# Two attentions and a mixture of experts on one core: the join of the attentions put into attention 1, memsets put off, and attention 1 written out

## The chip, the core and the metric

The kernel runs on one core of a Trainium2 chip. The core has TensorE (PE, matmuls; its weight loads are shown as PEld), VectorE (DVE), ScalarE (ACT), GpSimd (POOL) and SyncE (SP, which here issues DMAs). Each engine works through its own instructions in program order and waits for others by semaphores. The metric is the device time of one execution in microseconds.

## The reference, cut to what matters

Everything is float32. The input x is 4 batches of 256 tokens of 256 elements.

```python
x = x + layernorm(attention1(layernorm(x)))      # 16 heads of 16, causal
x = x + layernorm(ffn(layernorm(x)))
def ffn(f):
    h = rmsnorm(f, ln1_w)
    # attention 2: 32 query heads of 128 on 4 key heads, rotary positions, causal
    x = f + softmax(mask(rope(h @ Wq) @ rope(h @ Wk).T / sqrt(128))) @ (h @ Wv) @ Wo
    t = rmsnorm(x, ln2_w)
    # 8 of 32 experts for each token, and a shared expert
    return x + moe(t) + shared(t)
```

## The kernel before

Products are kept exact to float32 by splitting each operand into a high and a low part, and `three` (L71) issues three matmuls for each product (L73, L74, L75). ACT makes the high part by a copy out of PSUM, DVE the low part by a subtraction.

Four blocks of the program follow each other, and all engines meet between two of them:

- `prepare` (L252 on): loads x and the weights, normalises x (`Norm`: `moments` on DVE at L142 to L150, `roots` on ACT at L164, `factors` on DVE at L170 and L173, `apply` on ACT at L185), turns tokens so that features are on partitions (`Turn`: transposes L212 on PE, high part L222 on ACT, low part L231 on DVE) into `act_t`, and zeroes buffers on POOL (L303 to L318).
- attention 1 (`AttentionA`, tags `a_`): 8 iterations (a batch and half of its heads each) of 4 slots (a pair of heads each). The work of a slot is a software pipeline: scores of pair P, transposed probabilities of P-2, values of P-4, the output projection of P-5, and units (projections of the next iteration). Iterations 0, 1, 6 and 7 are written out; 2 to 5 are a loop (`Fori`) whose body holds two. Five slots of drain end it. From its third iteration on, a projection reads the turned tokens from `src_t`, into which SP copies a batch by DMA (L947).
- attention 2 (`AttentionB`, tags `b_`): 16 iterations (a key head and a batch) of 4 slots, all written out. A slot needs its queries three slots ahead: projection (PE), raw copy (ACT, L1119), exchange of halves by two DMAs (SP, L1127), rotation in two steps (POOL, L1147 and L1151), high part (ACT, L1156) and low part (DVE, L1161). SP first issues the weights of the next key head on the same queue (L1487).
- the experts, not touched.

Between the attentions stands the join, for each batch b: normalise attention 1's sum (statistics, then L185 on ACT), add it to x (L1639 on DVE), statistics of the new x, the feed-forward input in two scalings (POOL, L1680, keeps one in `acc` as what attention 2 is added to; ACT, L185, makes the other), and `Turn` into `act_t`. Before, all of this but the first statistics of batches 0 to 2 stands at the start of attention 2, in the order that `pipeline` gives, with attention 2's first projections laced in. The rows go into `prob`, so attention 2's probabilities must not come before them.

A sqrt and an exp need different tables in ACT, and the compiler puts an ACT_TABLE_LOAD before the first use after a change.

## Times and profile before

| | us |
|---|---|
| median of 3 runs | 960.92 (959.73 to 962.18) |
| the profiled execution | 961.15 |
| its span, first to last instruction | 959.1 |
| prepare, to the start of attention 1 | 25.4 |
| attention 1 | 25.4 to 182.7 |
| start of attention 2, to its first scores | 183.0 to 213.4 |
| attention 2 and the experts | 213.4 to 959.1 |

Busy over the whole span: PE 870.1 us (91%), DVE 624.5 (65%), ACT 569.9 (59%), POOL 456.0 (48%). These shares are means over stretches with different limits; a row for one stretch tells more. In a row of a timeline the first number is the start in us from the span's start, the second the time in us that the instructions took together, x their count, and the bracket the idle time of the engine before them and what ended it.

### The profile page before, as it was taken

Reading aid. Unit: us, or ns where it says so; the run is one execution under the profiler, and the core shown is the slowest. Engines: PE = TensorE matmul, PEld = TensorE weight load, DVE = VectorE, ACT = ScalarE, POOL = GpSimd, SP = SyncE. Lnnn points to the kernel's source line nnn. Section 1 sums busy time; section 2 is a strip of 40 time slices with the busy share of each in tenths; the row PEclk is TensorE's granted clock in tenths of the full one; section 3 lists DMA queues with packets and bytes.
Section 4 is the critical chain, followed back from the end, with each engine's and each line's share of the span. In section 5 each row is a group of like instructions: output and inputs, shape, how many; then the busy total and the mean of one; then the engine's idle time right before and its main releaser. Section 6 shows DMA issues by size and latency. Waiting matters only on the chain. (4 is left out here: it accounts for less than half of the span.)

```text
span 959.1 us, 18782 instructions
## 1 busy us (share of the span) xinstructions
PE 870.1 (91%) x6108; PEld 804.9 (84%) x6108; DVE 624.5 (65%) x1620; ACT 569.9 (59%) x1572; POOL 456.0 (48%) x480
## 2 busy tenths in 40 slices
PE   4699999467999999999999999978999999999994
PEld 2589899456999998999899999967888888888884
DVE  7366666656788788877778777765545444444546
ACT  4788888455776766667666676654443334333333
POOL 5633334156766776777766777720222222221221
PEclk9999999778999999999999999997999999999998
DMA  6000100311114111141111111200433333333321
GB/s 210 23 1 24 44 23 1 99 34 38 41 46 134 44 44 35 44 134 45 33 46 40 40 46 45 51 1 17 142 116 110 99 114 103 110 115 115 104 88 44
DMA packets 50246, 63.34 MB, mean 66 GB/s; under 512 B 5728, under 2 KB 36064, under 8 KB 50176
## 3 DMA queue, kind: packets, MB, share of 16 engines
q1 hardware_dynamic: 49088, 61.41, 21.9%
q10 hardware_dynamic: 1088, 1.05, 0.3%
q8 instruction: 37, 0.61, 0.3%
q14 instruction: 33, 0.27, 0.1%
HBM read 41.86 MB, written 1.18 MB: 45 GB/s over the span
## 5 line engine op out<-in xcount | busy, mean ns | idle before, releaser
L637 POOL TENSOR_TENSOR b_prob<-b_prob,b_rsum 128x256 f32<-128x256 f32 (+1 forms) x128 | 104.9, 840 | 111.0 <-DVE b_rsum L619 111.0
L73 PE MATMUL banks<-act_t,b_w 128*128 128x256 f32 (+1 forms) x392 | 130.1, 332 | 1.9 <-DVE moe_hid L1994 1.0
L75 PE MATMUL banks<-act_t,b_w 128*128 128x256 f32 (+1 forms) x392 | 128.0, 327 | 0.0
L74 PE MATMUL banks<-act_t,b_w 128*128 128x256 f32 (+1 forms) x392 | 127.9, 326 | 0.0
L1898 ACT ACTIVATE moe_hid<-banks 128x512 fp32r<-128x512 f32 x66 | 39.5, 598 | 124.2 <-DVE banks L1989 124.2
L1298 ACT ACTIVATE b_prob<-banks,b_negmax 128x128 f32<-128x128 f32 (+1 forms) x256 | 103.6, 417 | 14.1 <-DVE b_negmax L1285 14.0
L1982 DVE TENSOR_TENSOR moe_gated<-banks,moe_share 128x512 f32<-128x512 f32 x66 | 45.6, 691 | 85.4 <-PE banks L75 81.8
L1156 ACT ACTIVATE b_qt<-b_work 128x512 fp32r<-128x512 f32 x64 | 40.4, 632 | 90.0 <-POOL b_work L1151 90.0
L1151 POOL TENSOR_TENSOR b_work<-b_work 128x512 f32<-128x512 f32 x64 | 86.6, 1353 | 9.5 <-DVE b_work L1139 0.4
L637 POOL TENSOR_TENSOR a_prob<-a_prob,a_rsum 128x256 f32<-128x256 f32 x64 | 51.6, 828 | 81.4 <-DVE a_rsum L619 81.4
L1147 POOL TENSOR_TENSOR b_work<-b_work,rope_t 128x512 f32<-128x512 f32 x64 | 83.2, 1300 | 7.9 <-DMA b_work<-b_work 7.9
L1285 DVE CUSTOM_DVE_ANT_0 banks<-banks,mask_neg 128x128 f32<-128x128 f32 (+1 forms) x256 | 83.6, 387 | 3.5 <-PE banks L75 1.0
L73 PE MATMUL banks<-b_kt,b_qt 128*128 128x128 f32 (+1 forms) x256 | 76.2, 298 | 8.1 <-issue 6.2
L73 PEld LDWEIGHTS banks<-act_t,b_w 128*128 128x128 f32 x392 | 76.4, 195 | 7.1 <-DVE moe_hid L1994 1.2
L75 PEld LDWEIGHTS banks<-act_t,b_w 128*128 128x128 f32 x392 | 75.8, 193 | 6.1
L74 PEld LDWEIGHTS banks<-act_t,b_w 128*128 128x128 f32 x392 | 76.2, 194 | 4.8
L73 PE MATMUL banks<-b_w,b_ot 128*128 128x256 f32 x256 | 73.1, 286 | 5.6 <-DVE b_ot L1342 5.6
L1994 DVE TENSOR_TENSOR moe_hid<-banks,moe_hid 128x512 fp32r<-128x512 f32 x66 | 45.6, 692 | 45.3 <-ACT moe_hid L1898 45.3
L1342 DVE TENSOR_TENSOR b_ot<-banks,b_ot 128x512 fp32r<-128x512 f32 x64 | 44.1, 689 | 44.8 <-ACT b_ot L1337 44.7
L75 PE MATMUL banks<-b_w,b_ot 128*128 128x256 f32 x256 | 72.4, 283 | 0.0
L74 PE MATMUL banks<-b_w,b_ot 128*128 128x256 f32 x256 | 72.3, 283 | 0.0
L1945 POOL TENSOR_TENSOR b_w<-b_w_raw,b_w 128x512 fp32r<-128x512 f32 x16 | 20.8, 1298 | 106.8 <-ACT b_w L1884 106.8
(229 smaller groups left out, 3041.4 us busy)
## 6 DMA issues: line engine op xcount, KB each, us to landing
b_work<-b_work SPq DMA_DIRECT2D x128, 128.0 KB, 2.3
moe_share<-gates SPq DMA_DIRECT2D x32, 512.0 KB, 3.6
b_w_raw<-in_b_wq SPq DMA_DIRECT2D x4, 1024.0 KB, 5.4
b_w_raw<-in_b_wo SPq DMA_DIRECT2D x4, 1024.0 KB, 9.1
a_src_t<-act_t SPq DMA_DIRECT2D x5, 512.0 KB, 2.9
moe_w_raw<-in_wg SPq DMA_DIRECT2D x16, 128.0 KB, 2.2
moe_w_raw<-in_wu SPq DMA_DIRECT2D x16, 128.0 KB, 2.3
moe_w_raw<-in_wd SPq DMA_DIRECT2D x16, 128.0 KB, 2.2
```

The source lines that it names most:

```text
L73: nc.tensor.matmul(out, w_lo, m_hi, start=start, stop=False, skip_group_check=skip)
L74: nc.tensor.matmul(out, w_hi, m_lo, start=False, stop=False, skip_group_check=skip)
L75: return nc.tensor.matmul(out, w_hi, m_hi, start=False, stop=stop, skip_group_check=skip)
L637: last = self.m.nc.gpsimd.tensor_tensor(rows, rows, rsum[:, :, t:t + 1].to_broadcast([PART, 2, width]), ALU.mult)
L1147: nc.gpsimd.tensor_tensor(sin, sin, self.q_table(1), ALU.mult).then_inc(self.sin_ready, 1)
L1151: nc.gpsimd.tensor_tensor(total, total, self.swp[:, P % 2, :], ALU.add).then_inc(self.q_added, 1)
L1156: self.m.nc.scalar.activation(self.qt[:, P % PAIRS, 0, :], self.cos_part[:, P % 2, :], ACT.Copy).then_inc(self.qt_hi, 1)
L1285: last = nc.vector.tensor_tensor_reduce(row, row, m.mask_neg[:, SEQ - width:SEQ], 1.0, -NEG, ALU.add, ALU.min, accum_out=self.negmax[:, p ...
L1298: last = nc.scalar.activation(self.prob[:, p, h, lo:lo + width], m.s_ps[:, h, lo:lo + width], ACT.Exp, bias=self.negmax[:, p % 2, t, h:h + ...
L1342: self.m.nc.vector.tensor_tensor(self.ot[:, p % 2, 1, :], self.m.o_ps[:], self.ot[:, p % 2, 0, :].bitcast(F32), ALU.subtract).then_inc(sel ...
L1982: nc.vector.tensor_tensor(gated[n][:], gu[n][1], share[par][:, n * half:(n + 1) * half], ALU.mult).then_inc(gated_done, 1)
L1994: nc.vector.tensor_tensor(hid[n][:, 1, :], gu[n][0], hid[n][:, 0, :].bitcast(F32), ALU.subtract).then_inc(hid_ready, 1)
```

## The change

It consists of four edits.

1. `prepare` zeroes only half of `q_stack` and the key stack. The rest of `q_stack` and the value buffer `v` are zeroed by POOL at the start of attention 1, and ACT waits for them (`zeroed`) before it first writes there.
2. The join is split up. Batches 0 and 1 are done within attention 1: `after(k)` is called behind each slot on each engine, k counting from -32 at the first slot of iteration 0 to -1 at the last of iteration 7, and 0 to 4 in the drain. Their rows lie in `q_stack` and the normalisation of attention 1's sum is POOL's for them. Batches 2 and 3 begin at attention 2's start and end in its slots 0 to 2 (the entries `"first"`); `Turn` uses banks 6 and 7 for them instead of 2 and 3.
3. Attention 1's loop is written out.
4. Its projections read `act_t` directly; `src_t` and the copies are gone.

```diff
-            nc.gpsimd.memset(m.b_w[:, 2 * B_W:4 * B_W].bitcast(F32), 0.0)
-            nc.gpsimd.memset(m.q_stack[:].bitcast(F32), 0.0)
+
+            nc.gpsimd.memset(m.q_stack[:, 0:NTT * HPI * PART].bitcast(F32), 0.0)
+            k_at = 2 * B_W + 2 * NTT * HPI * PART
+            nc.gpsimd.memset(m.b_w[:, k_at:k_at + NTT * HPI * STACK].bitcast(F32), 0.0)
...
-    COPIED = 3
-
     def src(self, it, part, c, t):
-        at = part * NC * SEQ + c * SEQ + t * PART
-        if isinstance(it, int) and it < self.COPIED:
-            at += self.batch(it) * SLOT
-            return self.m.act_t[:, at:at + PART]
-        return self.src_t[:, at:at + PART]
-
-    def wait_src(self, pe, it):
-        if not (isinstance(it, int) and it < self.COPIED):
-            pe.wait_ge(self.src_loaded, 16 * (it - self.COPIED + 1))
+        at = self.batch(it) * SLOT + part * NC * SEQ + c * SEQ + t * PART
+        return self.m.act_t[:, at:at + PART]
 
     def unit_bank(self, it, u):
...
-    def run(self, eng, slot, middles, after=None):
-
-
-        for it in range(2):
-            for p in range(PAIRS):
-                slot(eng, it, p)
-        for first, last in middles:
-            self.splitting = last <= self.ITS - NB
-            with eng.Fori(first // self.UNROLL, last // self.UNROLL) as step:
-                for k in range(self.UNROLL):
-                    self.parity = k
-                    for p in range(PAIRS):
-                        slot(eng, step * self.UNROLL + k, p)
-        for it in range(middles[-1][1], self.ITS):
+    def run(self, eng, slot, after=None):
+
+
+        for it in range(self.ITS):
             for p in range(PAIRS):
                 slot(eng, it, p, units=it < self.ITS - 1)
+                if after:
+                    after(PAIRS * (it - self.ITS) + p)
         for k in range(self.DRAIN):
...
+        if it == 0:
+            wait(act, self.zeroed, 1)
...
+            if it == 1:
+                wait(act, self.zeroed, 2)
...
+            nc.gpsimd.memset(self.v.rearrange("p a t h n -> p (a t h n)").bitcast(F32), 0.0).then_inc(self.zeroed, 1)
+            nc.gpsimd.memset(m.q_stack[:, NTT * HPI * PART:].bitcast(F32), 0.0).then_inc(self.zeroed, 1)
             nc.gpsimd.memset(m.acc[:], 0.0).then_inc(self.y_added, 1)
...
+            def after(k):
+
+                if k == -5:
+                    pool.wait_ge(self.qt_full, PAIRS * (self.ITS - 1))
+                    join.pool_attention(pool, 0)
+                if k == -4:
+                    join.pool_attention(pool, 1)
+                if k in (2, 3):
+                    join.gpsimd(pool, k - 2)
+
+            self.run(pool, self.slot_pool, after)
...
+            def after(k):
+                if k in (3, 4):
+                    if k == 3:
+                        pe.wait_ge(self.exp_done, 2 * PAIRS * self.ITS)
+                    join.turn.tensor(pe, k - 3)
+
+            self.run(pe, self.slot_pe, after)
...
+            def after(k):
+                if k == -6:
+                    m.norm_a.roots(act, 0)
+                    m.norm_a.roots(act, 1)
+                if k == 0:
+                    join.norm_f.roots(act, 0)
+                    join.norm_f.roots(act, 1)
+                    m.norm_a.roots(act, 2)
+                if k in (1, 2):
+                    join.act_input(act, k - 1)
+                if k in (3, 4):
+                    join.turn.scalar(act, k - 3)
+
+            self.run(act, self.slot_act, after)
...
+            def after(k):
+
+                if k in (-8, -7, -2):
+                    b = {-8: 0, -7: 1, -2: 2}[k]
+                    m.norm_a.moments(dve, b, lambda t: acc[:, t, :], arrived)
+                if k == -6:
+                    m.norm_a.factors(dve, 0)
+                    m.norm_a.factors(dve, 1)
+                if k in (-4, -3):
+                    join.dve_add(dve, k + 4)
+                if k == 1:
+                    join.norm_f.factors(dve, 0)
+                    join.norm_f.factors(dve, 1)
+                    m.norm_a.factors(dve, 2)
+                if k == 4:
+                    join.turn.vector(dve, 0)
+
+            self.run(dve, self.slot_dve, after)
+            join.turn.vector(dve, 1)
...
+        if it < NB:
+            wait(pe, self.join.turn.lo_done, it + 1)
...
+        if P == 0:
+            wait(pe, self.join.turn.lo_done, 3)
...
-            self.join.gpsimd(pool, 0)
-            self.join.gpsimd(pool, 1)
             self.pool_kv(pool, 0, self.KV0)
             self.pool_kv(pool, 0, self.KV1)
-            self.join.gpsimd(pool, 2)
             self.pool_rotate(pool, 0)
-            self.join.gpsimd(pool, 3)
             self.pool_rotate(pool, 1)
-            self.slots(pool, self.slot_pool, {})
+            join = lambda b: self.join.gpsimd(pool, b)
+            self.slots(pool, self.slot_pool, {("first", 0): ((join, 2),), ("first", 1): ((join, 3),)})
...
-            turn.tensor(pe, 0)
-            pe.wait_ge(turn.lo_done, 1)
             self.pe_kv(pe, 0, self.KV0)
-            turn.tensor(pe, 1)
             self.pe_kv(pe, 0, self.KV1)
             self.pe_queries(pe, 0)
-            turn.tensor(pe, 2)
             self.pe_queries(pe, 1)
-            turn.tensor(pe, 3)
             self.pe_kv(pe, 0, self.KT)
             self.pe_queries(pe, 2)
-            pe.wait_ge(turn.lo_done, NB)
+
+            def turn_h(b):
+                pe.wait_ge(*((self.raw_ready, 2) if b == 2 else (self.k_raw_ready, NTT)))
+                turn.tensor(pe, b)
...
+            join = self.join
+            join.act_attention(act, 2)
+            self.act_kv(act, 0, self.KV0)
+            m.norm_a.roots(act, 3)
+            self.act_kv(act, 0, self.KV1)
+            join.norm_f.roots(act, 2)
+            self.act_raw(act, 0)
+            join.act_attention(act, 3)
+            self.act_raw(act, 1)
+            join.act_input(act, 2)
+            self.act_kv(act, 0, self.KT)
+            join.norm_f.roots(act, 3)
+            m.load_table(act, ACT.Exp)
+            self.act_queries(act, 0)
             self.act_raw(act, 2)
-            self.act_queries(act, 0)
+            turn_h = lambda b: join.turn.scalar(act, b)
+            input_h = lambda b: join.act_input(act, b)
 
...
+                ("first", 0): ((input_h, 3),), ("first", 1): ((turn_h, 2),), ("first", 2): ((turn_h, 3),),
...
+            m.norm_a.moments(dve, 3, lambda t: join.acc[:, t, :])
+            join.dve_add(dve, 2)
+            self.dve_kv(dve, 0, self.KV0)
+            m.norm_a.factors(dve, 3)
+            self.dve_kv(dve, 0, self.KV1)
+            join.norm_f.factors(dve, 2)
+            self.dve_cos(dve, 0)
+            join.dve_add(dve, 3)
+            self.dve_cos(dve, 1)
+            self.dve_kv(dve, 0, self.KT)
+            join.norm_f.factors(dve, 3)
             self.dve_queries(dve, 0)
             self.dve_cos(dve, 2)
+            turn_h = lambda b: join.turn.vector(dve, b)
 
...
+    def pool_attention(self, pool, b):
+
+        pool.wait_ge(self.norm_a.ready, b + 1)
+        for t in self.tiles(b):
+            last = self.m.nc.gpsimd.tensor_scalar(self.rows[:, t, :], self.acc[:, t, :],
+                                                  self.norm_a.factor[:, 0, t:t + 1],
+                                                  self.norm_a.shift[:, 0, t:t + 1], ALU.mult, ALU.add)
+        last.then_inc(self.attn_ready, 1)
+
+    def act_attention(self, act, b):
+        for t in self.tiles(b):
+            last = self.norm_a.apply(act, self.rows[:, t, :], self.acc[:, t, :], t)
+        last.then_inc(self.attn_ready, 1)
+
+    def dve_add(self, dve, b):
+        x, rows = self.m.x, slice(NTT * b, NTT * (b + 1))
+        dve.wait_ge(self.attn_ready, b + 1)
+        self.m.nc.vector.tensor_tensor(x[:, rows, :], x[:, rows, :], self.rows[:, rows, :],
+                                       ALU.add).then_inc(self.x1_ready, 1)
+        self.norm_f.moments(dve, b, lambda t: x[:, t, :], lambda t: dve.wait_ge(self.x1_ready, b + 1))
+
+    def act_input(self, act, b):
+        for t in self.tiles(b):
+            last = self.norm_f.apply(act, self.rows[:, t, :], self.m.x[:, t, :], t, 1)
+        last.then_inc(self.turn.rows_ready, 1)
 
```

On ACT, in the last slots of iteration 6 of attention 1, this stood before (L571 is the exp, L913 a unit's stacks, L885 the queries):

```order
L571 ACTIVATE a_prob,a_sums<-banks,a_negmax 128x256
L913 ACTIVATE a_q_stack<-banks 128x8x32
L913 ACTIVATE b_w<-banks 128x16x16
L580 ACTIVATE a_prob_t<-banks 128x768
L885 ACTIVATE a_qt<-banks 128x512
L571 ACTIVATE a_prob,a_sums<-banks,a_negmax 128x128
```

And this stands there now (L564 is the exp, L901 the stacks, L871 the queries, L164 the roots of the layer norm's denominators):

```order
L564 ACTIVATE a_prob,a_sums<-banks,a_negmax 128x256
L901 ACTIVATE a_q_stack<-banks 128x8x32
L901 ACTIVATE b_w<-banks 128x16x16
L164 ACT_TABLE_LOAD
L164 ACTIVATE ln_a_den<-ln_a_den 128x2 x2
L573 ACTIVATE a_prob_t<-banks 128x768
L871 ACTIVATE a_qt<-banks 128x512
L564 ACT_TABLE_LOAD
L564 ACTIVATE a_prob,a_sums<-banks,a_negmax 128x128
```

Two table loads and two roots have come between two slots' exps.

On PE, from the last projection of attention 1 (`a_wo`) into attention 2, this stood before (the branches are the border of the blocks; `b_prob` holds the rows of the join; the first `b_w<-act_t` products are attention 2's first projection):

```order
L75 MATMUL banks<-a_wo,a_ot 128x256
L2111 UNCONDITIONAL_BRANCH
L1514 UNCONDITIONAL_BRANCH
L212 MATMUL banks<-ident,b_prob 128x128 x4
L73 MATMUL banks<-b_w,act_t 128x256
L74 MATMUL banks<-b_w,act_t 128x256
L75 MATMUL banks<-b_w,act_t 128x256
L73 MATMUL banks<-b_w,act_t 128x256
L74 MATMUL banks<-b_w,act_t 128x256
L75 MATMUL banks<-b_w,act_t 128x256
L212 MATMUL banks<-ident,b_prob 128x128 x4
L73 MATMUL banks<-b_w,act_t 128x256
```

And now:

```order
L75 MATMUL banks<-a_wo,a_ot 128x256
L212 MATMUL banks<-ident,a_q_stack 128x128 x4
L2137 UNCONDITIONAL_BRANCH
L1540 UNCONDITIONAL_BRANCH
L73 MATMUL banks<-b_w,act_t 128x256
L74 MATMUL banks<-b_w,act_t 128x256
L75 MATMUL banks<-b_w,act_t 128x256
L73 MATMUL banks<-b_w,act_t 128x256
L74 MATMUL banks<-b_w,act_t 128x256
L75 MATMUL banks<-b_w,act_t 128x256
L73 MATMUL banks<-b_w,act_t 128x256
```

The transposes of batches 0 and 1 have moved ahead of the border, and those of 2 and 3 behind the first slots of attention 2; nothing of the join stands between the first projections any more.

## Rows read from the trace of the kernel before

**Rows 1.** Stretches: from:to, length, busy us of each engine (instructions), granted clock, DMA share, GB/s.
```profile
67.30:84.70 17.40, 16.84 (x138) 16.04 (x138) 11.17 (x34) 15.16 (x49) 6.38 (x9) 1.00 0.08 32
...
137.00:154.30 17.30, 16.85 (x138) 16.04 (x138) 11.18 (x34) 15.19 (x49) 6.47 (x9) 1.00 0.00 1
...
168.90:182.60 13.70, 9.88 (x75) 8.78 (x73) 9.71 (x31) 4.79 (x10) 2.66 (x4) 0.92 0.01 2
183.00:213.40 30.40, 13.34 (x67) 12.02 (x67) 17.98 (x62) 17.58 (x41) 12.57 (x16) 0.65 0.34 100
213.40:238.40 25.00, 18.25 (x122) 17.65 (x123) 16.80 (x49) 13.67 (x47) 16.83 (x18) 0.80 0.16 38
```

**Rows 2.** Timeline and line L150, preparation: POOL's memsets, DVE and ACT.
```profile
2.81 7.79 POOL L317 MEMSET b_w<- 128x9216 f32 x1
10.53 3.52 POOL L318 MEMSET a_q_stack<- 128x4096 f32 x1
...
4.67 0.43 DVE L142 BATCH_NORM_STATS2 pre_ln_x_stats<-x 128x6 f32<-128x256 f32 x1 [0.70 <-DMA x<-in_x]
...
5.35 8.72 DVE L150 TENSOR_SCALAR pre_ln_x_den<-pre_ln_x_mv 128x2 f32<-128x2 f32 x1
...
L150 DVE TENSOR_SCALAR pre_ln_x_den<-pre_ln_x_mv x4: 168/170/8719, 5.4 to 17.4; 128x2 f32<-128x2 f32 x4
...
14.88 1.09 ACT L185 ACTIVATE acc<-x,pre_ln_x_shift,pre_ln_x_factor 128x256 f32<-128x256 f32 x2
```

**Rows 3.** Loads: x's fourth DMA with its landing, then SP's last weights with theirs.
```profile
L287 SPq DMA_DIRECT2D x<-in_x x1: 433/433/433, 2.2 to 2.2; - x1
...
DMA to landing us min/median/max: 5.0/5.0/5.0
...
8.52 0.49 SPq L297 DMA_DIRECT2D b_w_raw<-in_b_wo  x1
...
b_w_raw<-in_b_wo SPq DMA_DIRECT2D x1, 1024.0 KB, 9.2
```

**Rows 4.** Timeline, start of attention 1: POOL and PE.
```profile
25.37 1.81 POOL L957 MEMSET acc<- 128x2048 f32 x1 [11.32 <-POOLq L257]
...
34.73 5.21 POOL L962 TENSOR_TENSOR b_w<-b_w_raw,b_w 128x1152 fp32r<-128x1152 f32 x2 [1.50 <-ACT b_w L979]
...
44.31 0.82 PE L518 MATMUL banks<-ident,a_prob 128*128 128x128 f32 x6
```

**Rows 5.** One batch's moments as a stretch, a table load, the join's add.
```profile
171.74:173.00 1.26, 1.26 (x14) 1.26 (x13) 1.19 (x6) 0.32 (x1) 1.20 (x2) 1.00 0.00 0
...
179.41 1.28 ACT L164 ACT_TABLE_LOAD   x1
...
184.17 0.69 DVE L1639 TENSOR_TENSOR x<-x,b_prob 128x512 f32<-128x512 f32 x1
```

**Rows 6.** Timeline, start of attention 2: PE, ACT, POOL, PE.
```profile
192.26 0.58 PE L73 MATMUL banks<-b_w,act_t 128*128 128x256 f32 x1 [2.75 <-DVE act_t L231]
...
194.51 0.56 PE L73 MATMUL banks<-b_w,act_t 128*128 128x256 f32 x1
...
200.63 0.58 ACT L1119 ACTIVATE b_work<-banks 128x512 f32<-128x512 f32 x1
...
204.18 1.26 POOL L1147 TENSOR_TENSOR b_work<-b_work,rope_t 128x512 f32<-128x512 f32 x1 [4.00 <-DMA b_work<-b_work]
...
213.37 0.30 PE L73 MATMUL banks<-b_kt,b_qt 128*128 128x128 f32 x1 [2.47 <-issue]
```

**Rows 7.** SP's last weights for the second key head, issue and landing.
```profile
184.47 1.18 SPq L1487 DMA_DIRECT2D b_w_raw<-in_b_wo  x1
...
b_w_raw<-in_b_wo SPq DMA_DIRECT2D x1, 1024.0 KB, 8.1
```

**Rows 8.** Timeline, DVE: the low part of the first queries.
```profile
212.09 1.18 DVE L1161 TENSOR_TENSOR b_qt<-b_work,b_qt 128x512 fp32r<-128x512 f32 x1 [1.78 <-ACT b_qt L1156]
```

**Rows 9.** Line L496 from 60 to 160 us: what its engine was idle for.
```profile
  issue: 4.5, 8
```

More of the change, by code:

```diff
@@ L536, in late_unit @@
         if p == 0:
-            known = isinstance(it, int) and not 0 < it < self.ITS
+            known = not 0 < it < self.ITS
             return None if known or len(self.schedule[-1]) < 2 else (it, self.schedule[-1][1])
@@ L937, in build @@
         nc, m = self.m.nc, self.m
-        middles = ((2, self.ITS - 2),)
+        join = m.join
+        join.use_rows(m.q_stack[:, 0:NT * D].bitcast(F32))
         block = self.ctx.enter_context(nc.Block())
@@ L989, in _ @@
             split_weights(3)
-            self.run(act, self.slot_act, middles)
-            for b in range(NB - 1):
-                m.norm_a.roots(act, b)
+            def after(k):
[11 more added lines that the diff above has]
+            self.run(act, self.slot_act, after)
         @block.vector
@@ L1002, in arrived @@
                 dve.wait_ge(self.y_added, 2 * (t // NTT + 1) + 1)
-            def moments(k):
-                if k < NB - 1:
-                    m.norm_a.moments(dve, k, lambda t: acc[:, t, :], arrived)
-            self.run(dve, self.slot_dve, middles, moments)
-            for b in range(NB - 1):
-                m.norm_a.factors(dve, b)
+            def after(k):
[15 more added lines that the diff above has]
+            join.turn.vector(dve, 1)
 W_DMAS = 4
@@ L1074, in __init__ @@
         self.kt_hi = sem("kt_hi")
-        rows = self.prob[:].rearrange("p a h n -> p (a h n)")[:, 0:NT * D]
-        self.join = Join(m, ctx, rows.rearrange("p (t d) -> p t d", t=NT))
+        rows = self.prob[:].rearrange("p a h n -> p (a h n)")[:, PAIRS * 2 * PCOLS - NT * D:]
+        self.join = m.join
+        self.join.use_rows(rows)
         rows = work[:].rearrange("p a n -> p (a n)")[:, 0:NT * D].rearrange("p (t d) -> p t d", t=NT)
@@ L1320, in pe_project @@
         wait(pe, self.o_ready, P + 1)
+        if P == 0:
+            wait(pe, self.join.turn.lo_done, NB)
         if p == 0:
@@ L1474, in slots @@
             slot(eng, P)
-            for stage, b in plan.get(P - self.STAGES, ()):
+            for stage, b in plan.get(P - self.STAGES, ()) + plan.get(("first", P), ()):
                 stage(b)
@@ L1657, in scalar, with use_rows @@
-    def scalar(self, act):
-        def attention(b):
-            for t in range(NTT * b, NTT * (b + 1)):
-                last = self.norm_a.apply(act, self.rows[:, t, :], self.acc[:, t, :], t)
-            last.then_inc(self.attn_ready, 1)
-        def ffn_input(b):
-            for t in range(NTT * b, NTT * (b + 1)):
-                last = self.norm_f.apply(act, self.rows[:, t, :], self.m.x[:, t, :], t, 1)
-            last.then_inc(self.turn.rows_ready, 1)
-        def last_attention(s):
-            if s == 0:
-                self.norm_a.roots(act, NB - 1)
-        return ((3, lambda b: self.turn.scalar(act, b)), (2, ffn_input),
-                (1, lambda b: self.norm_f.roots(act, b)), (0, attention), (0, last_attention))
+    def use_rows(self, rows):
+        self.rows = self.turn.src = rows.rearrange("p (t d) -> p t d", t=NT)
@@ new lines, in tiles @@
+    def tiles(self, b):
+        return range(NTT * b, NTT * (b + 1))
+    def pool_attention(self, pool, b):
[5 more added lines that the diff above has]
+        last.then_inc(self.attn_ready, 1)
@@ L2103, in program @@
         m.norm_a = Norm(m, ctx, "ln_a")
+        m.join = Join(m, ctx)
         with ExitStack() as early:
```

72 lines of the change are left out of this document (13 added, 59 removed).

## The prediction

> **What bounds the kernel now.** Read the table of stretches first [rows 1]. In attention 1's loop (67.3 to 84.7 us is one iteration) PE is busy 16.84 of 17.4 us; it is the bound there, with ACT at 15.16 close behind. Three stretches are not bound by any engine. The preparation comes first: attention 1 begins only at 25.37 us [rows 4]. The drain of attention 1 (168.9 to 182.6) has PE busy for 9.88 of 13.7. And from 183.0 to 213.4, between the attentions, PE works 13.34 of 30.4 us at a mean granted clock of 0.65: a chain of small steps is being followed and no engine is full. The change touches all three. The steady part of attention 2 and the experts it leaves alone.
>
> Second, the timeline of the preparation [rows 2]. DVE's L150, a 128x2 tensor_scalar, begins at 5.35 and takes 8.72 us, where the others of that line there take 0.17. It ends at 14.07, and POOL's two memsets of L317 and L318, back to back from 2.81, end at 14.05. So DVE stood still for POOL. ACT's first normalisation (L185) then starts at 14.88, 0.81 behind, and from there ACT and DVE have hardly a gap until attention 1 begins.
>
> Third, the timeline between the attentions [rows 6]. Attention 2's first projection is at 192.26: PE has waited there for the turned tokens of batch 0, whose normalisations, add and transposes all come after the block begins. Its first scores come at 213.37, which is 30.3 us after the block's first instructions at 183.05.
>
> **The sum, part by part.** All of it against the profiled execution: 961.15 us, of which the span is 959.1. That is 0.2 over the median of 960.92.
>
> *Memsets.* L317 goes from 9216 columns to 1024, L318 from 4096 to 2048. At 7.79 us for 9216 and 3.52 for 4096 [rows 2] that is 0.87 and 1.76 us, so POOL is done at 2.81 + 2.63 = 5.4 and L150 is free at once. What is late next is x: DVE's second pair of moments comes before its first factors in program order, and needs tile 3. That was issued at 2.24 and landed 5.0 us later [rows 3], at 7.2. A bn_stats of 0.43 and the 0.81 us of before bring L185 to 8.5 instead of 14.88: 6.4 us. Cover to check: SP's wait for the raw weights of attention 2. The last was issued at 8.52 and took 9.2 us, so landed at 17.7 [rows 3]; attention 1 would now begin at 25.37 - 6.4 = 19.0, 1.3 behind it. Bounds: nothing, and 8.7 if DVE never waited for x. Taken: **-6.4**.
>
> *The memsets put off.* Attention 1 on POOL now begins with 4096 columns (3.5 us) and 2048 (1.8) ahead of the acc memset (1.81). Behind them in POOL's queue wait the four splits (L962, 2.6 us each) and the first normalisation, L637. Before, the splits were over at 34.73 + 5.21 = 39.94, 14.6 us into the block [rows 4]. Now that is 7.1 + 4 x 2.6 = 17.5; the normalisation behind takes two steps of 0.8 and ends at 19.1, and PE took up the transposes of its rows (L518) at 44.31, 18.9 into the block. Bounds 0 and 3.0; taken **+0.4**. The two new waits of ACT for these memsets come in slots 1 and 3, at 16 us and later, when they have been done for 11 us: 0.
>
> *The loop.* An iteration in the loop takes 17.4; the straight-line iteration 6 (137.0 to 154.3) takes 17.3 with the same work [rows 1]. Four iterations give **-0.3**. The five copies of 512 KB are SP's alone and PE never waited for one: 0.
>
> *Join work put into attention 1's iterations 6 and 7.* ACT gets two sqrt tables' worth: a table load to sqrt, two roots of 0.2, and a load back to exp; a load is 1.28 us [rows 5]: 2.96 in all. ACT has (17.3 - 15.19)/4 = 0.5 us free in a slot [rows 1], and the next exps release the next scores, so PE is held 2.4. DVE gets moments(0) and (1) in slots of iteration 6, 1.2 us each [rows 5]. DVE is busy 11.18 of 17.3 there, so they fit: 0.2 together. In iteration 7 it gets two adds with moments, 0.69 + 1.3 = 2.0 us each, and moments(2). DVE has (17.3 - 11.18)/4 = 1.5 free in a slot, and less there, since the last slots have no unit of a next iteration and are shorter; I take 1.3: 2 x 0.7, and 0.2 for locking against POOL. Bounds: 0, and all of it in a row, 2.96 + 8.3 = 11.3. Taken **+4.2**.
>
> *The drain.* It had DVE's three moments and now has 0.9 us of factors on DVE, ACT's two act_input (1.09, as L185 in [rows 2]) and two turns. ACT is busy for 4.79 of the 13.7 us there [rows 1], in steps that wait for PE, so only one of them sticks out, by 0.5. DVE ended the stretch with 1.4 us of factors behind its last add; it now ends it with two turns, which I put at 0.9 each, and the second's wait for ACT: +1.0. Taken **+1.5**, bounds 0 and 3.5.
>
> *The start of attention 2.* Batch 0 is turned already. PE runs KV0 and KV1 at once, six matmuls each, then both queries, twelve each. At the lower clock six take 1.4 us: before, the second six began at 194.51 with a granted clock of 0.65 over the stretch [rows 1, 6]. So KV0, KV1 and the first query end 5.7 us into the block, and ACT's raw copy (0.58) at 6.3. The swap DMA of it took 200.63 + 0.58 to 204.18, 2.97 us. It would be there at 9.3, but SP has sent 2.36 MB of weights ahead of it on the same queue: issued up to 184.47 and 8.1 us to land [rows 7], which is 9.5 in. I take 10.0. POOL's rotation is two steps of 1.26 with 0.15 between: 12.7. ACT's copy 0.5, DVE's split 1.2, for it meets POOL's next rotation as it did at 212.09, where it took 1.18 [rows 8]; the add of the same width takes 0.69 alone [rows 5]. ACT's queue is done by then: from 6.3 the attention of batch 3 (1.1), the second raw copy once PE's second query is done (8.9), act_input(2) (10.0), the K copy and a root (10.6) and the exp load (12.0). Scores at 14.7 instead of 30.3: **-15.6**. Bounds -12 (the swap a whole weight transfer late, ACT's exp table late too) and -18 (no queueing, PE at full clock).
>
> *The ramp.* Joins 2 and 3 are partly inside slots 0 to 2: ACT +1.09 and two turns, DVE two turns, POOL two joins of two steps, which cost it less than a rotation each, some 1.5 us. POOL is the tight one: it is busy 16.83 of 25.0 us in the ramp [rows 1], and nearly all of the rest lies before its first normalisation. The first join falls in that free part, the second does not: +1.5. The third query's swap starts 1.1 us later against the scores than before: +1.1. Bounds 0 and 6. Taken **+2.7**.
>
> Sum: -6.4 + 0.4 - 0.3 + 4.2 + 1.5 - 15.6 + 2.7 = -13.5, so 961.15 - 13.5 = 947.6; the forecast is **947.7 us**.
>
> **Two rules beside the trace.** The row: a DVE tensor_scalar held until a POOL memset ended, while bn_stats and bn_aggr ran under the same memset [rows 2]. The Trainium skill (SBUF — State Buffer, "SBUF: two separate sides") says that GpSimd and VectorE share a port pair as an exclusive lock; a VectorE operation in a two-port mode waits for any GpSimd operation, one with two SBUF inputs only for a GpSimd operation that reads SBUF. By that rule the memsets moved into attention 1 hold nobody, since DVE's steps there read PSUM (the trace has no such meeting), and the sum stands; it also speaks against the change, since the new tensor_scalars of POOL do read SBUF and meet the adds of iteration 7. The other: the trace has a table load at 1.28 us [rows 5]. The Trainium skill (ScalarE: Activation LUTs, "Table sets: the hidden batching unit") gives about 2.7 us. By its figure the two new loads would cost 2.8 more and the result be 950.5; the trace's own duration is used.
>
> **Rivals.**
> R1, the inserted work is paid in full. Attention 1 has no slack that is of use, since ACT and PE are both nearly full; for: ACT at 88% [rows 1]; against: DVE at 65%. Then +11.3 for +4.2: 954.8.
> R2, it is covered. ACT's 2.96 less a slot's slack and what PE still had to do costs 1.9, DVE's nothing, and the ramp, where PE works 18.25 of 25.0 us [rows 1], takes its additions free: -2.3 and -2.7, so 942.7.
> R3, the change doesn't do in the preparation what it could. DVE's 8.72 us are a load's, not the memset's; for: x lands in just that time; against: the end agrees within 0.02 us with the memset's [rows 2], and L150 needs tiles 0 and 1 alone, whose statistics were done. Then the 6.4 are missing: 954.1.
> R4, slower. Written-out code feeds PE worse than a loop: PE's queue in iterations 2 to 5, sixteen slots. For: before L496 PE sat idle 4.5 us in 8 cases with nothing but issue to name [rows 9]. Against: iteration 6 is written out and takes 17.3. It decides from (13.5 + 2.9)/16 = 1.0 us a slot; at 1.2 the time is 961.15 - 13.5 + 19.2 = 966.9.
>
> **Numbers.** Forecast 0.60, R1 0.17, R2 0.13, R3 0.05, R4 0.05. The range takes in R1, R2 and R3 without their far ends: 941 to 955. No change means within 0.3% (2.9 us), about what a measurement of this kernel can tell. The first four are all faster; of R4's 0.05 I put 0.02 within and 0.03 slower. Faster 0.95.
>
> **What would show it.** L150 at 0.17 us, and attention 1's first projection at 19.0 instead of 25.41. An iteration of 17.3 for 2 to 5. Two table loads of 1.28 in iteration 6, with PE idle about 2.4 us behind them; above 6 in all it is R1. Attention 1's end near 182.5 (the gains and costs up to there nearly cancel: -6.4 + 0.4 - 0.3 + 4.2 + 1.5 = -0.6). The first scores of attention 2 14.7 us after its block begins, near 197.3; if later, the swap's landing or POOL will be what is waited for. From slot 4 on everything as before, 13.5 us earlier. I am wrong if L150 still ends with x, or if the first scores stay more than 20 us behind the block's start.

## The result, and the profile after

The changed kernel takes 949.6 us (median, 949.2 to 950.03) against 961.27 in runs of before beside it: ratio 0.988, 95% interval 0.9863 to 0.9897. The forecast of 947.7 was 1.9 too low and the time is well inside the range of 941 to 955. The profiled execution has a span of 948.2 (before 959.1).

The stretches of the changed kernel (columns as in [rows 1]): an iteration of attention 1, iteration 6, the slots of iteration 7, the start of attention 2, and the ramp (its first slots, as in [rows 1]).

```profile
60.20:77.50 17.30, 16.80 (x138) 16.02 (x139) 11.18 (x34) 15.16 (x49) 6.48 (x9) 1.00 0.01 2
129.30:149.60 20.30, 16.89 (x139) 15.92 (x140) 13.82 (x48) 17.88 (x53) 7.63 (x11) 0.97 0.01 2
149.60:164.20 14.60, 13.62 (x96) 13.19 (x96) 12.08 (x39) 10.15 (x33) 6.05 (x9) 0.80 0.00 1
182.66:199.44 16.78, 8.13 (x50) 7.66 (x50) 9.17 (x33) 8.28 (x20) 6.11 (x8) 0.70 0.58 173
199.44:225.70 26.26, 19.43 (x131) 18.82 (x131) 17.43 (x53) 16.68 (x54) 21.25 (x23) 0.76 0.18 41
```

The start of attention 2 is 16.8 us where it was 30.4, and PE there still works only half of the time at a clock of 0.70. Iteration 6 is 20.3 us, 3 more than the 17.3 of one in the middle, with the same work of PE (16.89 us): the inserted work is paid there. In the slots of iteration 7 the granted clock is 0.80.

The preparation in the timeline of the changed kernel: the first of POOL's two memsets (the other ends at 5.49), DVE, ACT, PE's first projection of attention 1 and POOL's first memset there. They answer to [rows 2, 4].

```profile
2.80 1.80 POOL L318 MEMSET a_q_stack<- 128x2048 f32 x1
...
5.41 0.17 DVE L150 TENSOR_SCALAR pre_ln_x_den<-pre_ln_x_mv 128x2 f32<-128x2 f32 x1
...
7.71 0.43 DVE L142 BATCH_NORM_STATS2 pre_ln_x_stats<-x 128x6 f32<-128x256 f32 x1 [1.47 <-DMA x<-in_x]
...
8.85 1.09 ACT L185 ACTIVATE acc<-x,pre_ln_x_shift,pre_ln_x_factor 128x256 f32<-128x256 f32 x2 [1.65 <-DVE pre_ln_x_shift L173]
...
19.39 0.66 PE L73 MATMUL banks<-a_wqkv,act_t 128*128 128x384 f32 x1 [2.11 <-PEq L257]
...
19.35 3.51 POOL L936 MEMSET b_w<- 128x4096 f32 x1 [13.86 <-POOLq L257]
```

L150 takes 0.17 us instead of 8.72. What is late next is the load of x, as forecast: DVE waits 1.47 us for its fourth tile. ACT's first normalisation is 6.0 us earlier, and so is attention 1.

Iterations 6 and 7 in the timeline: ACT with its two table loads, PE in the slot behind them and at the start of iteration 7, and DVE and POOL in the last slot.

```profile
142.92 1.28 ACT L164 ACT_TABLE_LOAD   x1
144.21 0.30 ACT L164 ACTIVATE ln_a_den<-ln_a_den 128x2 f32<-128x2 f32 x2
...
145.71 1.28 ACT L564 ACT_TABLE_LOAD   x1
...
147.16 0.85 PE L511 MATMUL banks<-ident,a_prob 128*128 128x128 f32 x6 [1.25 <-DVE a_prob_t L636]
149.58 0.37 PE L489 MATMUL banks<-mask,ident 128*128 128x256 bf16 x1 [1.57 <-ACT b_w L905]
...
164.30 0.82 DVE L150 TENSOR_SCALAR ln_a_den<-ln_a_mv 128x2 f32<-128x2 f32 x1
...
163.49 1.61 POOL L630 TENSOR_TENSOR a_prob<-a_prob,a_rsum 128x256 f32<-128x256 f32 x2 [2.18 <-DVE a_rsum L612]
```

The loads and roots are 2.9 us of ACT's time, and PE waits 1.25 and 1.57 behind them, 2.8 us together. Not all of that is theirs: without them PE still waits 0.55 and 0.28 at the same two places (`e3_no_roots` below).

The start of attention 2, to be held against [rows 6 to 8]: SP's last weights with their landing, the first exchange (the row begins with the first unit's two DMAs), ACT's raw copy, POOL, ACT, DVE, PE.

```profile
184.08 0.90 SPq L1516 DMA_DIRECT2D b_w_raw<-in_b_wo  x1
...
b_w_raw<-in_b_wo SPq DMA_DIRECT2D x1, 1024.0 KB, 10.2
...
188.04 2.14 SPq L1150 DMA_DIRECT2D b_work<-b_work  x3
...
187.41 0.60 ACT L1142 ACTIVATE b_work<-banks 128x512 f32<-128x512 f32 x1 [1.10 <-PE banks L75]
...
194.95 1.26 POOL L1170 TENSOR_TENSOR b_work<-b_work,rope_t 128x512 f32<-128x512 f32 x1 [7.33 <-DMA b_work<-b_work]
...
197.65 0.63 ACT L1179 ACTIVATE b_qt<-b_work 128x512 fp32r<-128x512 f32 x1 [4.91 <-POOL b_work L1174]
198.31 1.08 DVE L1184 TENSOR_TENSOR b_qt<-b_work,b_qt 128x512 fp32r<-128x512 f32 x1 [6.05 <-ACT b_qt L1179]
...
199.44 0.47 PE L73 MATMUL banks<-b_kt,b_qt 128*128 128x128 f32 x1 [5.77 <-DVE b_qt L1184]
```

Read from the bottom up, this is one chain: PE waits for DVE, DVE for ACT, ACT for POOL, and POOL for the exchange of halves. From the end of the raw copy (188.01) to POOL's rotation (194.95) are 6.9 us; before they were 2.97. The weights issued at 184.08 landed at 194.3. The first scores are 16.8 us into the block.

### The profile page after: what moved, and what is told of

The parts are those of the page before. It is cut to its first block and busy times, and to the rows that moved or that the text cites. A ratio compares the mean times of both kernels' runs of the same rounds, so it can differ in the third digit from the quotient of the medians.

```text
span 948.2 us, 18579 instructions
## 1 busy us (share of the span) xinstructions
PE 868.7 (92%) x6108; PEld 803.5 (85%) x6108; DVE 615.3 (65%) x1620; ACT 569.7 (60%) x1570; POOL 455.1 (48%) x486
## 5 line engine op out<-in xcount | busy, mean ns | idle before, releaser
L73 PE MATMUL banks<-act_t,b_w 128*128 128x256 f32 (+1 forms) x392 | 128.8, 329 | 4.4 <-DVE b_work L1162 3.2
L74 PE MATMUL banks<-act_t,b_w 128*128 128x256 f32 (+1 forms) x392 | 126.8, 323 | 0.0
L75 PE MATMUL banks<-act_t,b_w 128*128 128x256 f32 (+1 forms) x392 | 126.5, 323 | 0.0
L73 PE MATMUL banks<-b_kt,b_qt 128*128 128x128 f32 (+1 forms) x256 | 77.2, 302 | 10.9 <-DVE b_qt L1184 6.4
L73 PEld LDWEIGHTS banks<-act_t,b_w 128*128 128x128 f32 x392 | 75.2, 192 | 9.5 <-issue 3.6
L75 PEld LDWEIGHTS banks<-act_t,b_w 128*128 128x128 f32 x392 | 74.9, 191 | 6.0
L74 PEld LDWEIGHTS banks<-act_t,b_w 128*128 128x128 f32 x392 | 74.9, 191 | 4.7
L73 PE MATMUL banks<-b_w,b_ot 128*128 128x256 f32 x256 | 72.6, 284 | 5.6 <-DVE b_ot L1371 5.6
L74 PE MATMUL banks<-b_kt,b_qt 128*128 128x128 f32 (+1 forms) x256 | 72.3, 282 | 0.0
L75 PE MATMUL banks<-b_w,b_ot 128*128 128x256 f32 x256 | 71.8, 281 | 0.0
```

The costliest lines, as they stand in the source:

```text
L73: nc.tensor.matmul(out, w_lo, m_hi, start=start, stop=False, skip_group_check=skip)
L74: nc.tensor.matmul(out, w_hi, m_lo, start=False, stop=False, skip_group_check=skip)
L75: return nc.tensor.matmul(out, w_hi, m_hi, start=False, stop=stop, skip_group_check=skip)
```

## The experiments

Ratios are to runs of before on the same chip. Times are medians; a number after "under the changed kernel" is the difference to the 950.18 us of the first experiment. "Changed kernel" is the kernel after the change, and a mark is the start of a named instruction.

### The changed kernel again

No edit; the base for the others.

> The changed kernel itself, beside the others on one chip: 11 to 12 us under the kernel before, 949.6 within 1.

Measured: 950.18 us (948.88 to 951.7), ratio 0.9872 (0.9852 to 0.9892). In its profile, iterations 6 and 7 to the last scores, and everything behind attention 2's last scores, to be held against the second fence, before, for the same two:

```profile
131.50:164.60 33.10, 27.84 (x234) 26.49 (x234) 25.86 (x87) 28.14 (x86) 13.70 (x19) 1.00 0.01 1
...
614.80:949.20 334.40, 311.96 (x1779) 274.07 (x1777) 172.30 (x326) 130.60 (x253) 73.60 (x74) 0.96 0.29 92
```

```profile
137.00:165.50 28.50, 27.74 (x232) 26.60 (x233) 18.45 (x55) 25.11 (x82) 10.73 (x15) 1.00 0.01 1
626.70:959.10 332.40, 310.25 (x1779) 272.44 (x1777) 172.78 (x326) 130.58 (x253) 73.94 (x74) 0.97 0.29 92
```

At full clock the inserted work costs 33.1 - 28.5 = 4.6 us. In the first profile of the changed kernel the same two iterations took 34.9: the granted clock was half there from 148.5 to 155.4. The two executions differ by nothing else, so the 1.8 us between them are the clock's, and they are not in every execution.

### Memsets, alone and taken back

`e1_memsets_back`: the changed kernel, with the memsets whole in the preparation again.

```diff
-            nc.gpsimd.memset(m.q_stack[:, 0:NTT * HPI * PART].bitcast(F32), 0.0)
-            k_at = 2 * B_W + 2 * NTT * HPI * PART
-            nc.gpsimd.memset(m.b_w[:, k_at:k_at + NTT * HPI * STACK].bitcast(F32), 0.0)
+            nc.gpsimd.memset(m.b_w[:, 2 * B_W:4 * B_W].bitcast(F32), 0.0)
+            nc.gpsimd.memset(m.q_stack[:].bitcast(F32), 0.0)
...
-            nc.gpsimd.memset(m.q_stack[:, NTT * HPI * PART:].bitcast(F32), 0.0).then_inc(self.zeroed, 1)
+            pool.sem_inc(self.zeroed, 2)
```

> The changed kernel with the two whole memsets back in the preparation and none of them in attention 1. Theory (a DVE tensor_scalar waits for POOL's memset): 5.5 to 6.5 us over the changed kernel, attention 1 begins at 25.4, L150 again takes 8.7 us. Rival (x's loads set that stretch, and the change's gain there is from elsewhere): under 1 us over it.

Measured: 953.89 us, ratio 0.9918 (0.9901 to 0.9934): 3.7 over the changed kernel, less than the 5.5 to 6.5 expected. L150 is held again:

```profile
5.38 8.68 DVE L150 TENSOR_SCALAR pre_ln_x_den<-pre_ln_x_mv 128x2 f32<-128x2 f32 x1
...
2.81 7.78 POOL L318 MEMSET b_w<- 128x9216 f32 x1
10.52 3.52 POOL L319 MEMSET a_q_stack<- 128x4096 f32 x1
...
137.00:170.10 33.10, 27.76 (x232) 26.46 (x233) 25.79 (x87) 28.19 (x86) 13.69 (x19) 1.00 0.01 1
619.40:951.30 331.90, 309.56 (x1779) 271.89 (x1777) 172.37 (x326) 130.64 (x253) 73.77 (x74) 0.97 0.29 92
```

Attention 1's first projection is at 25.40, and attention 2's last scores begin at 619.4, 4.6 to 4.8 later than in the two profiles of the changed kernel (614.8 and 614.6). Behind them this kernel takes 331.9 us where those took 334.4 and 333.6. So the start is as forecast, 5.6 to 6.0 us; 1.0 to 1.2 of it are gone by the last scores, most of that between attention 2's first scores and its last (414.2 us here, 415.0 and 415.1 there), and the rest of the difference goes in the experts.

`e5_memsets_only`: before, with the same memsets put off and nothing else.

```diff
-            nc.gpsimd.memset(m.b_w[:, 2 * B_W:4 * B_W].bitcast(F32), 0.0)
-            nc.gpsimd.memset(m.q_stack[:].bitcast(F32), 0.0)
+            nc.gpsimd.memset(m.q_stack[:, 0:NTT * HPI * PART].bitcast(F32), 0.0)
...
+            wait(act, self.zeroed, 1)
...
+            nc.gpsimd.memset(m.q_stack[:, NTT * HPI * PART:].bitcast(F32), 0.0).then_inc(self.zeroed, 1)
```

> The kernel before with the memsets put off and nothing else. Theory: the preparation's 6.0 us arrive in full, since nothing behind depends on the time: 5.5 to 6.5 us less than before. Rival (POOL's late first normalisation gives some back): 3 to 5 less.

Measured: 955.5 us, ratio 0.9925 (0.9906 to 0.9944), 6.0 under before. Its rows:

```profile
5.46 0.17 DVE L150 TENSOR_SCALAR pre_ln_x_den<-pre_ln_x_mv 128x2 f32<-128x2 f32 x1
...
8.41 1.09 ACT L185 ACTIVATE acc<-x,pre_ln_x_shift,pre_ln_x_factor 128x256 f32<-128x256 f32 x2 [1.12 <-DVE pre_ln_x_shift L173]
...
61.80:131.40 69.60, 67.37 (x552) 64.13 (x552) 44.80 (x136) 60.67 (x196) 25.64 (x33) 1.00 0.08 31
```

L185 comes 6.5 us earlier than before. The row of four iterations of the loop is for the next experiment.

### The loop written out, alone

`e4_loop_only`: before, with attention 1 written out and its projections reading `act_t` itself.

```diff
-            with eng.Fori(first // self.UNROLL, last // self.UNROLL) as step:
...
+        for it in range(self.ITS):
...
-                sp.dma_start(self.src_t[:].bitcast(F32), self.m.act_t[:, bass.ds(b * SLOT, SLOT)].bitcast(F32),
```

> The kernel before with attention 1 written out and its projections reading the turned tokens directly, nothing else. Theory: an iteration takes 17.25 instead of 17.4 us, so 0.5 to 1 us less than the kernel before. Rival R4 (written-out code feeds PE worse): slower than before.

Measured: 962.12 us, ratio 0.9999 (0.9989 to 1.0009): no difference, where 0.5 to 1 us less was expected. The four middle iterations:

```profile
68.20:137.40 69.20, 67.35 (x554) 64.16 (x554) 44.79 (x136) 60.72 (x196) 25.81 (x33) 1.00 0.01 1
```

69.2 us written out, 69.6 in the loop. PE's work is the same. The 0.4 us are the loop's turns and the copies together, which this edit does not separate, and they do not show in the whole time. No slot became slower, which ends rival R4.

### The two table loads

`e3_no_roots`: the changed kernel without ACT's square roots of batches 0 and 1 in iteration 6. It leaves out part of the computation: the factor of those two batches is the reciprocal of the variance, not of its root.

```diff
-        dve.wait_ge(self.root_ready, b + 1)
+        if b < self.rootless:
+            dve.wait_ge(self.var_ready, b + 1)
+        else:
+            dve.wait_ge(self.root_ready, b + 1 - self.rootless)
...
-                if k == -6:
-                    m.norm_a.roots(act, 0)
-                    m.norm_a.roots(act, 1)
```

> The changed kernel without the square roots of batches 0 and 1 in attention 1 (the factor is the reciprocal of the variance there), so without the two table loads in iteration 6; nothing else is left out. Theory A (the two loads and what hangs on them hold PE): 2.4 us less than the changed kernel if the table loads alone count, 4 to 5 less if the half clock from 148.5 to 155.4 us comes from the same pause and goes with it. Rival (DVE's adds and moments hold those slots): under 1 us less, and the slots of iteration 7 stay at 5 us and more.

Measured: 946.77 us, ratio 0.9839 (0.9821 to 0.9856), 3.4 under the changed kernel beside it.

```profile
129.80:161.20 31.40, 27.87 (x233) 26.53 (x234) 26.11 (x87) 25.50 (x82) 13.86 (x19) 1.00 0.01 2
```

At full clock the two iterations take 31.4 instead of 33.1: the loads and roots are 1.7 of the 4.6 us. By slots (starts of the mask matmul, at full clock in both) the one with the loads takes 4.8 instead of 6.8, and one later 0.3 more. Some of the rest of the 3.4 us is the clock, it seems. Of the seven profiles of kernels with the two loads, four have a stretch of half clock at the start of iteration 7: of 6.9 us in the first of the changed kernel and of 6.8 in `e8_adds_late` (mean clock of the two iterations 0.90 in both), of 3.4 us in `e2_weights_early` and `e10_other_queue` (0.95). The five profiles without the loads, three of them with no inserted work at all, have none. Three profiles with the loads have none either, so this is a tendency only, and 1.8 us is all that the longest such stretch cost; what is left of the 3.4 us was not traced to a place.

### The adds moved behind iteration 7

`e8_adds_late`: the changed kernel with both adds and their moments behind the last slot.

```diff
-                if k in (-4, -3):
-                    join.dve_add(dve, k + 4)
+                if k == 0:
+                    join.dve_add(dve, 0)
+                    join.dve_add(dve, 1)
```

> The changed kernel with the adds and moments of batches 0 and 1 moved from iteration 7's first two slots into the drain's first. Theory (they stick out of DVE's slack by some 1.5 us where they are): iteration 7 gets 1 to 2 us shorter, but the drain longer by more, so 1 to 4 us over the changed kernel. Rival (they are free where they are): iteration 7 unchanged.

Measured: 953.26 us, ratio 0.9912 (0.9894 to 0.9931), 3.1 to 3.7 over the two medians of the changed kernel. From attention 1's last scores to attention 2's first projection, the changed kernel and this one:

```profile
164.20:182.84 18.64, 13.17 (x107) 11.90 (x104) 11.48 (x31) 11.45 (x29) 6.29 (x9) 1.00 0.00 1
```

```profile
164.10:186.44 22.34, 14.61 (x106) 13.48 (x104) 15.19 (x45) 11.65 (x31) 6.80 (x9) 0.92 0.00 1
```

In iteration 7 the last two slots take 3.5 us each without the adds, and 4.3 and 4.2 with them in the second profile of the changed kernel, at full clock in both: the adds cost 1.6 there. In the drain they cost 3.7, at a mean clock of 0.92 instead of 1.00, with DVE busy 3.7 us longer. So DVE's slack in attention 1 is real, though not whole. The two places make 2.1 of the 3.1 to 3.7 us; the rest was not traced.

### The first exchange and the weights

The start of attention 2 was the largest miss, so four kernels bear on it. `e2_weights_early`: the changed kernel, with the raw weights of the second key head sent in attention 1, once POOL has split the first ones.

```diff
+            sp.wait_ge(m.raw_free, 1)
+            for dst, src in group_weights(m, dram, 1):
+                sp.dma_start(dst, src).then_inc(m.w1_loaded, 16)
...
-            load_weights(1)
```

> The changed kernel with the raw weights of attention 2's second key head loaded within attention 1, once POOL has read the first ones, so that they are not on SP's queue ahead of the first exchanges of query halves. Theory (the first scores are late because the exchange lies behind 2.36 MB of weights): the exchange lands some 3 us after its raw copy instead of 6.9, the first scores come 13 us after the block begins instead of 16.8, and the time is 3 to 4 us less than the changed kernel's. Rival (POOL or ACT's exp table holds the first queries anyway): under 1 us less.

Measured: 945.32 us, ratio 0.9829 (0.9813 to 0.9844), 4.9 under the changed kernel.

```profile
189.00 0.60 ACT L1146 ACTIVATE b_work<-banks 128x512 f32<-128x512 f32 x1 [1.09 <-PE banks L75]
...
192.60 1.27 POOL L1174 TENSOR_TENSOR b_work<-b_work,rope_t 128x512 f32<-128x512 f32 x1 [3.06 <-DMA b_work<-b_work]
...
184.74:197.14 12.40, 9.15 (x51) 8.65 (x51) 9.14 (x33) 8.41 (x20) 6.17 (x8) 0.72 0.19 44
```

Copy to rotation is 3.0 us, first projection to first scores 12.4 instead of 16.6.

`e9_weights_behind`: the weights stay in attention 2, behind the exchanges of the first two units.

```diff
-            load_weights(1)
             for P in range(self.STAGES):
+                if P == 2:
+                    load_weights(1)
```

> The changed kernel, but SP sends the four weight transfers of the second key head (2.36 MB) behind the exchanges of the first two units of queries instead of ahead of them. In the changed kernel the first exchange is issued at 188.0 and POOL's rotation that needs it begins 6.9 us later, with the weights on the same queue; with the weights sent already in attention 1 it was 3.0. Theory (the exchange stands behind the weights in the order of one queue, or shares the DMA engines with them): the first exchange takes 3 us, the first scores come 12.4 us after the first projection instead of 16.6, and the third unit's exchange, which now stands behind the weights, is late instead, so that the ramp gives back 2 to 4 of the 4.2: 946 to 949. Rival (it was the order of SP's own steps, or what the weights do to PE and ACT later): first exchange still 5 us or more, time as the changed kernel, 949.9.

Measured: 945.25 us, ratio 0.9833 (0.9807 to 0.9859). POOL's rotations of the first and of the third unit, SP's issue of the third's exchange, and the two stretches to the first scores and of the ramp:

```profile
190.86 1.27 POOL L1170 TENSOR_TENSOR b_work<-b_work,rope_t 128x512 f32<-128x512 f32 x1 [3.41 <-DMA b_work<-b_work]
...
201.81 1.29 POOL L1170 TENSOR_TENSOR b_work<-b_work,rope_t 128x512 f32<-128x512 f32 x1 [5.36 <-DMA b_work<-b_work]
...
194.72 1.11 SPq L1150 DMA_DIRECT2D b_work<-b_work  x2
...
182.66:195.37 12.71, 7.89 (x51) 7.48 (x51) 9.09 (x33) 8.22 (x20) 6.13 (x8) 0.87 0.45 129
195.37:223.70 28.33, 22.09 (x131) 21.38 (x131) 17.31 (x53) 16.77 (x54) 20.72 (x23) 0.71 0.30 82
```

First scores after 12.7 us instead of 16.6, and the third exchange takes 7.1 in place of the first: the ramp is 28.3 us against 26.3 (at a mean clock of 0.71 against 0.76), so 2 of the 3.9 are given back. The time is a little under the 946 to 949 of the theory, but not all of the 4.9 us is the weights' doing. At attention 2's last scores this kernel is only 2.6 to 2.8 us ahead of the two profiles of the changed kernel (612.0), and behind them it takes 331.3 us for their 333.6 and 334.4. `e2_weights_early` is 4.0 to 4.2 ahead there (610.6), though its attention 1 began 0.6 to 1.0 later.

`e10_other_queue`: the same weights at the block's start, but from ACT's queue.

```diff
-            load_weights(1)
...
             join.act_attention(act, 2)
+            act.wait_ge(self.w_ready, 4)
+            for dst, src in group_weights(m, dram, 1):
+                act.dma_start(dst, src).then_inc(self.w_loaded, 16)
```

> The changed kernel, but ACT sends the same four weight transfers, from its own queue, at the same place (behind its first normalisation of the block, about 2 us later than SP did). Rival A, the order within one queue: an exchange on SP's queue passes the weights, 3 us as without them, first scores 12.4 to 13.5 us after the first projection, time 945.5 to 947. Rival B, the DMA engines are shared whatever the queue: the exchange still takes 5 to 7 us, first scores 16 to 18 us after the first projection, time 949 to 952. ACT's four issues cost it about 2 us at a place where it waits for PE; I expect them to add under 0.5.

Measured: 949.16 us, ratio 0.986 (0.9833 to 0.9887), not told apart from the changed kernel.

```profile
185.42 0.86 ACTq L1576 DMA_DIRECT2D b_w_raw<-in_b_wo  x1
...
190.21 2.15 SPq L1150 DMA_DIRECT2D b_work<-b_work  x3
...
b_w_raw<-in_b_wo ACTq DMA_DIRECT2D x1, 1024.0 KB, 10.0
...
196.06 1.27 POOL L1170 TENSOR_TENSOR b_work<-b_work,rope_t 128x512 f32<-128x512 f32 x1 [6.91 <-DMA b_work<-b_work]
...
186.00:194.00 8.00, 5.56 (x32) 5.36 (x31) 5.96 (x23) 5.28 (x15) 1.92 (x4) 0.71 1.03 323
184.09:200.56 16.47, 10.28 (x51) 9.78 (x51) 9.29 (x33) 8.22 (x20) 6.14 (x8) 0.71 0.59 177
```

SP issues the first exchange at 190.21, so from another queue the weights hold it for 5.9 us all the same, and it ends with them (185.42 + 10.0 = 195.4; POOL goes on at 196.06). So the order within one queue is not what holds it. From 186 to 194 the 16 DMA engines are busy throughout, with a share of 1.03 (1.08 in the changed kernel from 186 to 192), and in `e2_weights_early`, where the exchange takes 3.0 us, the share is 0.39 from 189.6 to 192.6. That points to the DMA engines, which both queues share.

`e7_both`: `e2_weights_early` and `e3_no_roots` together; like the latter it leaves out the roots of batches 0 and 1. It asks whether the two losses are independent.

> The changed kernel with both edits, the early weights and no square roots of batches 0 and 1 in attention 1 (the factor is the reciprocal of the variance there). If the two costs are independent, the sum of what each gave: 942 to 944 us if both theories hold.

Measured: 943.17 us, ratio 0.9803 (0.9783 to 0.9822): 7.0 under the changed kernel, of 8.3 if the two added up.

```profile
130.80:162.10 31.30, 27.75 (x232) 26.41 (x233) 26.06 (x87) 25.55 (x82) 13.77 (x19) 1.00 0.01 2
180.84:193.60 12.76, 8.04 (x51) 7.53 (x51) 9.12 (x33) 8.11 (x20) 6.14 (x8) 0.77 0.18 43
```

Both local savings are there, 31.3 us and 12.8 (12.4 in `e2_weights_early`). What does not add up comes later: from attention 2's first scores to its last this kernel takes 415.6 us and `e2_weights_early` 413.5, and why stays open.

## Why the prediction was right, step by step

The terms against the two profiles of the changed kernel (first and second; each is the shift of a mark against before, from the start of the one stretch to the next):

| term | forecast | measured |
|---|---|---|
| preparation | -6.4 | -6.0, -5.6 |
| start of attention 1 to iteration 2 | +0.4 | -1.1, +0.7 |
| loop, four iterations | -0.3 | -0.6, -0.6 |
| join work in iterations 6 and 7 | +4.2 | +6.4, +4.6 |
| drain | +1.5 | +0.9, +0.9 |
| start of attention 2 | -15.6 | -13.5, -13.6 |
| ramp, and attention 2 behind it | +2.7 | +1.8, +1.7 |
| experts | 0 | +1.2, +2.0 |
| sum | -13.5 | -10.9, -9.9 |

*Memsets.* The mechanism holds, shown by L150 in three kernels and by 6.0 us in the one that has nothing else. The 0.4 to 0.8 less than forecast are x's landing: DVE read its fourth tile at 7.71 and 8.09 in the two profiles, not 7.2. R3 is out.

*The memsets put off.* They cost nothing, where I had put 0.4. `e1_memsets_back` has none of them in attention 1 and takes 42.65 us from its first projection to iteration 2, the second profile of the changed kernel 42.68, each at a mean clock of 0.88. The -1.1 and +0.7 of the table are not this term: PE is busy for 33.6 us of that stretch in before and for 32.5 and 35.3 in the two profiles, with 224 or 225 matmuls in each, so they lie in how much of PE's work fell into half clock (mean clock 0.96, 0.96 and 0.88).

*The loop.* Right in sign and as small as forecast; R4 is out by the ratio of 0.9999.

*Iterations 6 and 7.* The step is right, 4.6 at full clock against 4.2. Its parts: loads and roots 1.7 (2.4 forecast), the adds 1.6 (1.6 with their locking), and 1.3 for all the rest, where I had put 0.2 with DVE's time to spare as the reason. Of these 1.3, 0.8 are in the slot that holds moments(1): it takes 5.0 us instead of 4.2, with and without the table loads: ACT's exps wait there 0.94 us for DVE's maxima (L605), and PE 0.59 for DVE's low part (L636). So DVE's average slack did not hide them. Moments(0), a slot earlier, cost nothing. What I had not in the sum is the half clock that follows in some executions. R1, all paid in full, would have been 11.3: it is out. R2, all covered, is out too.

*The drain.* DVE's two turns cost 0.9, less than 1.5. Had the adds stood there, 3.7 more.

*The start of attention 2.* The failed step is "It would be there at 9.3, but SP has sent 2.36 MB of weights ahead of it on the same queue: issued up to 184.47 and 8.1 us to land [rows 7], which is 9.5 in. I take 10.0." The mechanism was the right one and its size wrong: POOL got the exchange 12.3 into the block (194.95 - 182.66). The 8.1 us were a landing with no exchange beside it; with the exchanges the same transfer took 10.2, and landed 11.6 into the block instead of 9.5. All behind it went as forecast, 4.5 us from rotation to scores against 4.7 (of which the steps named made 4.4). ACT's exp load was done at 192.5 and bound nothing.

*The experts.* I had them unchanged, and their instructions are. But behind the last scores before, `e1`, `e4` and `e5` take 331.9 to 332.6 us with one half-clock stretch of 13.7 us beside the one in which all of them end, and the changed kernel 333.6 and 334.4 with a further one of 3.4 and 6.8 about 20 us after the last scores (633.2 to 636.6 in the first). That also accounts for the sums that did not close: memsets alone -6.0 and all the rest -7.9 (`e1`) would be -13.9, measured -11.7. At the last scores they do close: -5.0 and -7.3 against -12.1. The first profile's two added stretches, the one in the experts and the one of iteration 7, have these rows:

```profile
633.20:636.60 3.40, 3.40 (x15) 3.11 (x14) 0.19 (x2) 0.00 (x0) 0.00 (x0) 0.50 0.00 0
148.50:155.40 6.90, 5.82 (x28) 5.75 (x29) 4.26 (x11) 4.99 (x17) 3.98 (x7) 0.51 0.01 2
```

PE is busy all through the first of them, at 0.50. Before it, from 629.8 to 633.2, PE had been busy for 1.62 of 3.4 us at full clock. Why the clock falls there in these kernels and not in `e1` and `e10`, whose instructions there are the same, stays open. The other kernels that have it (`e2`, `e3`, `e7`, `e8`, `e9`) range from 331.3 to 333.4, so its price is not settled either.

*The whole.* The forecast has too little time for the start of attention 2, iterations 6 and 7, the preparation and the experts, and too much for the ramp, the drain, the memsets put off and the loop. These misses cancel in part, so that the total came within 1.9 us is in part luck.

The version that is faster than both kernels and computes the same: `e2_weights_early`, 945.3 us, or `e9_weights_behind`, with one call moved, 945.25; their ratios to before are 0.9829 and 0.9833. At attention 2's last scores the former is 1.4 us ahead of the latter.

## What to carry to other kernels

When a chain of small steps is brought forward, look for what it now meets: here a 256 KB exchange that had run after the weights came beside them, and a landing time read where a transfer was alone was too short. Large loads with much slack go behind small ones that something waits for, or a phase earlier; another queue did not help. Work put into a full loop is paid by slots, not by an engine's average: a slot with 35% idle of an engine still grew by 0.8 us for 1.2 us of it. And the parts should be compared at a mark in the timeline before the end, since a stretch of half clock far behind the change moved the total by as much as one of its terms.

## What the runs showed of the hardware

- A DVE tensor_scalar of 128x2, 0.17 us elsewhere, took 8.72 and 8.68 us under POOL memsets, and 0.82 under two POOL tensor_tensors, of 1.61 us together, with the second of which it ended (164.30 + 0.82 and 163.49 + 1.61). The Trainium skill (SBUF — State Buffer, "SBUF: two separate sides") says that a VectorE operation in a two-port mode waits for any GpSimd operation; the trace agrees with that as to the waiting, and does not show ports or modes. The memsets put off meet six steps of DVE that read PSUM (22.48 to 24.76 in the first profile), and none is held: 0.28 and 0.29 us each, as before from 145.79 on, where POOL was idle.
- The small exchange and 2.36 MB of weights: 3.0 us alone, 6.9 behind the weights on one queue, 5.9 with the weights on another, at a DMA share of 1.08 and 1.03 while they ran.
- A table load took 1.28 us in every case, also amid full work, and PE was held by two of them and the roots for 1.7 us net. The Trainium skill (ScalarE: Activation LUTs, "What ACT_TABLE_LOAD costs") has 1283 ns for the load and about 1380 for a drain with it, about 2.7 us for a switch. The trace agrees on the load, and shows no drain: the load at 142.92 begins as the copy before it ends (142.50 + 0.41), and the roots begin at its end (144.21). The measurement decides.
- After PE had waited 1.25 and 1.57 us in iteration 6, the granted clock was the lower of its two levels (1.2 instead of 2.4 GHz) from 148.5 to 155.4 in the first profile. In the second, waits of 1.23 and 1.58 at the same places left it full. Such a stretch cost 1.8 us between these two profiles.
